# Expert weights in a mixture-of-experts kernel: from selector matmuls to a DRAM scratch and spreading DMAs

## The chip, the cores and the metric

The kernel runs on one core of one Trainium2 chip. Its engines are TensorE (PE; its weight loads are listed as PEld), VectorE (DVE), ScalarE (ACT), GpSimd (POOL) and SyncE (SP, which here only issues DMAs). The metric is the device time of one execution in microseconds, of which lower is better.

## What is computed

A network of four layers, each a cross-attention block and a feed-forward block with gated residuals, over x of 16 x 128 tokens with 128 features (2048 tokens). The feed-forward blocks of layers 0, 2 and 3 route tokens to experts. Cut to what matters:

```python
scores = sigmoid(x @ gate_weight.T)          # layers 0 and 3; layer 2: softmax
topk_idx = top_k(masked(scores), TOP_K)      # layer 0: 16 experts, 4 chosen; layer 3: 32, 6; layer 2: 8, 2
topk_w = topk_w / (topk_w.sum(-1) + 1e-20) * 2.5
combine = zeros((T, E)).at[arange(T)[:, None], topk_idx].add(topk_w)
y = sum over e of combine[:, e] * down_e(act(up_e(xn)))      # and one shared expert in layers 0 and 3
x = x + tanh(gate) * y
```

Experts have 64 hidden features in layers 0 and 3 and 128 in layer 2. Layer 3 has a second up projection per expert (silu(gate) * up).

## The kernel before, in words

The program is a row of stages; each is a block in which every engine has its own instruction stream, and semaphores order the streams. The three routed stages are `feed_forward` (L1394) with the tags f0, f2 and f3. Features lie on the 128 partitions and tokens along the free dimension. The tokens form 4 groups (NG) of 512 (GT). A tile is 128 hidden features, so two experts in f0 and f3 and one in f2; a group has J tiles: 10 in f0 (8 routed, 2 shared), 8 in f2, 17 in f3 (16 routed, 1 shared). Work is counted by n = g * J + j, N = 40, 32 and 68.

TensorE's order is written out by hand (L1504 to L1523). First come the router's logits (L1259), then `ahead` up projections (20 in f0, 16 in f2 and f3; L1456, and L1461 for the second one of f3), during which VectorE chooses the experts (`Route.choose`, L1296). `turn_back(0)` then transposes the weights of group 0 to expert-major form. After that, step m of the loop issues up(m + ahead), select(m), turn_back(m) for m = 1, 2, 3, and down(m - 2) (L1491). The last `ahead` steps have no up projection; the text calls them the tail.

The chosen weights leave `choose` in float32 and are split into three bf16 parts (L1388 to L1391), so that matmuls in bf16 move them exactly. `turn_back` multiplies the parts by an identity (L1276, four matmuls a group into bank 7), ScalarE copies the result to `combt` (`keep`, L1293), and `select(n)` (L1471) multiplies a matrix of ones and zeros, `sels`, by `combt`: the bank 4 or 5 then holds, on each partition, the weight of the expert to which this hidden feature belongs. VectorE's `weigh` (L1568) multiplies that PSUM bank by the activated hidden tile in the `ring` and writes h3, a ring of three buffers, which the down projection reads; `weigh(c)` waits for the down projection (in f2 for POOL's addition) of tile c - 3.

ScalarE activates every up projection into the ring (L1531) and in f3 copies the second one to `u` (L1537). POOL multiplies the two in f3 (L1617). In f2 the down matrix is the same for all experts, so POOL adds the 8 weighted tiles of a group (`accumulate`, L1632, seven additions), and one down projection a group follows. After a group's last down projection VectorE adds to x (L1576), takes statistics (L1582, L1588), POOL computes 1/sqrt(var) (L1645 to L1650), VectorE normalises (L1597) and TensorE turns the result (L1500); in TensorE's order this turn stands three steps behind the down projection. f3, the last stage, has none of this but stores x from SyncE (L1670).

`sels` is built by POOL: for f0 in the stage of L430, for f2 and f3 in pieces inside the attention stages before (`selector_piece`, L1209).

Of the kernel before, what the change touches and what calls it, by code (L numbers as in the profile page):

```python
# [77 lines left out]
class Kernel:  # L78


    def __init__(self, nc, ctx, dram, out):
# [35 lines left out]
        self.sels = sb("sels", [P, 2048], BF16)  # L117
        self.combt = sb("combt", [P, T], BF16)
# [295 lines left out]
def l0_queries_keys_values(k, lat_t, ctxn_t, qn, kl, kc, v):  # L414
# [9 lines left out]
         ("proj", "sq", "total", "root", "guard", "inv", "scaled", "turn", "copied", "sel")}  # L424
# [5 lines left out]
    with nc.Block() as block:  # L430
# [3 lines left out]

        @block.gpsimd
        def _(pool):
            pool.memset(k.combt[:, :], 0.0).then_inc(S["sel"], 1)
            make_selectors(pool, k, 16, 64, S["sel"], 1)
# [258 lines left out]
def small_head_attention(k, tag, sub, names, bias_q, bias_k, bv, bo, mask_rows, set_mask, weights_of, selectors):  # L697
# [20 lines left out]
          "inv", "on", "out", "added", "stated", "xb", "sel")}  # L718
# [14 lines left out]
    with nc.Block() as block:  # L733
# [100 lines left out]
        def _(pool):  # L834
            xv = k.x[:, :].rearrange("p (b c) -> p b c", b=NB)
            pool.memset(vp[:, :, :], 0.0).then_inc(S["zero"], 1)
            for b in range(NB + 1):
# [22 lines left out]
                if b >= 5 and (b - 5) % 2 == 0 and b < 13:  # L860
                    selector_piece(pool, k, *selectors, S["sel"], (b - 5) // 2)
# [347 lines left out]
def selector_piece(pool, k, experts, width, sem, piece):  # L1209

    s = k.sels[:, 0:experts * width].rearrange("p (e c) -> p e c", c=width)
    if piece == 0:
        pool.memset(k.sels[:, 0:experts * width], 0.0).then_inc(sem, 1)
        return
    pool.wait_ge(sem, piece)
    pool.affine_select(out=s, in_=s, compare_op=ALU.not_equal, fill=1.0, base=-(piece - 1) * experts,
                       pattern=[[-1, experts], [0, width]], channel_multiplier=1).then_inc(sem, 1)


def make_selectors(pool, k, experts, width, sem, n):  # L1220
    s = k.sels[:, 0:experts * width].rearrange("p (e c) -> p e c", c=width)
    pool.memset(k.sels[:, 0:experts * width], 0.0).then_inc(sem, 1)
    for part in range(3):
        pool.wait_ge(sem, n + part + 1)
        pool.affine_select(out=s, in_=s, compare_op=ALU.not_equal, fill=1.0, base=-part * experts,
                           pattern=[[-1, experts], [0, width]], channel_multiplier=1).then_inc(sem, 1)


class Route:
# [4 lines left out]
    def __init__(self, k, a, tag, E, groups, top_groups, top, kind, gate_w, rbias=None, factor=1.0):  # L1234
# [7 lines left out]
        self.s, self.w, self.low = take(E), take(E), take(E)  # L1242
# [3 lines left out]
        if groups:  # L1246
# [5 lines left out]
        self.parts = a.take((3 * NB * E + 1) // 2).bitcast(BF16).rearrange("p (t q e) -> p t q e", t=NB, q=3)  # L1252
        self.S = {n: k.sem(f"{tag}_" + n) for n in
                  ("logit", "st", "turn", "chain", "shift", "exp", "parts", "turn2", "comb")}
# [35 lines left out]
    def keep(self, act, g):  # L1290
        k, S, rows = self.k, self.S, 3 * self.E
        act.wait_ge(S["turn2"], g + 1)
        act.activation(k.combt[0:rows, g * GT:(g + 1) * GT], k.bank[7][0:rows, :], ACT.Copy)\  # L1293
           .then_inc(S["comb"], 1)

    def choose(self, dve):  # L1296
        k, S, E, G, best = self.k, self.S, self.E, self.G, self.best
        s, v, w, low, tot, base, rep, parts = (self.s, self.v, self.w, self.low, self.tot, self.base, self.rep,
                                               self.parts)
# [94 lines left out]
def feed_forward(k, tag, sub, tiles, function, ahead, one_down=False, routing=None, spare=(), bias=None):  # L1394
# [53 lines left out]
    with nc.Block() as block:  # L1448
        @block.tensor
        def _(pe):  # L1450
# [437 lines left out]
```

## Time and profile before

| | us |
|---|---|
| median of 3 runs (lowest to highest) | 1316.79 (1315.12 to 1317.58) |
| the profiled execution, own time | 1312.83 |
| its span, first to last instruction | 1311.0 |
| PE busy | 1142.2 (87%) |
| DVE busy | 765.1 (58%) |
| ACT busy | 682.4 (52%) |
| POOL busy | 364.4 (28%) |

The profile is of one execution, and all its times are counted from the span's start. f0 lies at about 140 to 242 us, f2 at 879 to 971, f3 at 1108 to 1311. Durations of matmuls include the fill of the pipeline, so that those of neighbours overlap; float32 matmuls are listed as two records each. What an instruction waited for stands in brackets behind it: idle time of the engine, and what ended it.

### The profile page before, as it was taken

The page shows a single profiled execution, that of the slowest core. Times are in us where ns is not written, and L with a number is a line of the kernel's source. Part 1 is how long each engine was busy: PE and PEld are TensorE (multiplying, and loading weights), DVE is VectorE, ACT ScalarE, POOL GpSimd, SP SyncE. Part 2 cuts the span into 40 slices and gives each one's busy share as a digit, 9 for nine tenths or more (in the row PEclk, how much of TensorE's full clock was granted, in tenths as well). Part 3 has the DMA queues.
Part 4 walks back from the last instruction along what each step waited for, and adds up shares of the span by engine and source line. Part 5 has one row for each costly group of instructions (what it writes and reads, how often), then busy time and mean ns, then how long its engine had stood idle before and what let it go on. Part 6 is the DMA issues. An engine that isn't in the chain of part 4 may idle for free. (4 is left out here: it accounts for less than half of the span.)

```text
span 1311.0 us, 24476 instructions
## 1 busy us (share of the span) xinstructions
PE 1142.2 (87%) x9697; PEld 838.0 (64%) x9697; DVE 765.1 (58%) x1671; ACT 682.4 (52%) x1205; POOL 364.4 (28%) x340
## 2 busy tenths in 40 slices
PE   1778898489999999999998599969439997999998
PEld 0567367478888888888885366643225664466667
DVE  5858535465656565656553379964537996722224
ACT  1677630165666666666654166656116665644441
POOL 3200001222222323232322422203662320744441
PEclk9999899699999999999999789989768997999999
DMA  4500000100000000000000000000000000000000
GB/s 166 189 1 1 0 1 1 65 1 1 1 1 1 1 1 1 1 2 1 1 2 1 0 2 2 2 1 0 0 0 2 2 2 2 1 0 8 9 0 17
DMA packets 6526, 16.27 MB, mean 12 GB/s; under 512 B 1312, under 2 KB 3568, under 8 KB 5520
## 3 DMA queue, kind: packets, MB, share of 16 engines
q1 hardware_dynamic: 6416, 14.74, 3.1%
q8 instruction: 77, 1.26, 0.4%
q14 instruction: 33, 0.27, 0.1%
HBM read 13.69 MB, written 1.05 MB: 11 GB/s over the span
## 5 line engine op out<-in xcount | busy, mean ns | idle before, releaser
L1099 POOL TENSOR_TENSOR work<-work 128x1024 f32<-128x1024 f32 x64 | 121.3, 1896 | 302.4 <-DVE work L1177 302.4
L1164 DVE TENSOR_REDUCE work<-psum 128x8 f32<-128x1024 f32 x64 | 78.0, 1219 | 93.0 <-PE psum L1000 93.0
L1116 ACT ACTIVATE work<-work 128x1024 f32<-128x1024 f32 x64 | 67.4, 1053 | 98.3 <-DVE work L1168 98.3
L1175 DVE TENSOR_REDUCE work<-work 128x8 f32<-128x1024 f32 x64 | 77.3, 1208 | 68.2 <-ACT work L1116 68.2
L1491 PEld LDWEIGHTS psum<-w_down,work 128*128 128x128 f32 x768 | 99.5, 191 | 24.4 <-issue 21.7
L887 ACT ACTIVATE work<-psum 128x512 f32<-128x512 f32 x128 | 72.8, 596 | 67.0 <-PE psum L777 66.1
L1491 PE MATMUL psum<-w_down,work 128*128 128x128 f32 x768 | 100.6, 275 | 0.7 <-DVE x L1576 0.7
L1568 DVE TENSOR_TENSOR work<-psum,big 128x512 f32<-128x512 f32 x67 | 45.8, 688 | 87.5 <-PE psum L1471 85.5
L919 DVE TENSOR_REDUCE work<-psum 128x8 f32<-128x1024 f32 x64 | 75.4, 1219 | 32.9 <-PE psum L765 18.8
L777 PEld LDWEIGHTS psum<-ident,work 128*128 128x128 f32 x512 | 57.4, 143 | 43.9 <-issue 30.7
L1168 DVE TENSOR_TENSOR work<-psum,work 128x1024 f32<-128x1024 f32 x64 | 78.4, 1225 | 6.4
L777 PE MATMUL psum<-ident,work 128*128 128x128 f32 x512 | 76.0, 282 | 6.3 <-ACT work L887 6.0
L1000 PEld LDWEIGHTS psum<-work 64*128 64x128 f32 x1024 | 59.6, 188 | 24.4 <-issue 23.5
L926 DVE TENSOR_TENSOR work<-psum,work 128x1024 f32<-128x1024 f32 x64 | 75.0, 1213 | 0.0
L884 ACT ACTIVATE work<-work 128x1024 f32<-128x1024 f32 x64 | 65.5, 1052 | 14.0 <-DVE work L926 13.0
L1120 ACT ACTIVATE work<-psum 128x512 f32<-128x512 f32 x128 | 69.2, 598 | 2.3 <-PE psum L1015 2.3
L1015 PE MATMUL psum<-ident,work 128*128 128x128 f32 x512 | 66.4, 273 | 0.9 <-ACT work L1120 0.9
L1456 PE MATMUL psum<-xnt,ctx_tok 128*128 128x512 f32 x128 | 66.6, 602 | 0.0
L1000 PE MATMUL psum<-work 64*128 64x128 f32 x1024 | 65.8, 278 | 0.7 <-ACT work L1111 0.7
L1461 PE MATMUL psum<-xnt,big 128*128 128x512 f32 x128 | 65.8, 595 | 0.0
L1645 POOL TENSOR_SCALAR work<-work 128x4 f32<-128x4 f32 x12 | 2.7, 228 | 217.5 <-DVE work L1588 217.5
L1032 PE MATMUL psum<-work 128*64 128x128 f32 x1024 | 63.0, 276 | 0.1
(319 smaller groups left out, 2544.5 us busy)
## 6 DMA issues: line engine op xcount, KB each, us to landing
x<-in_x SPq DMA_DIRECT2D x1, 1024.0 KB, 4.8
ctx_tok<-in_ctx SPq DMA_DIRECT2D x1, 1024.0 KB, 6.8
ctxt<-in_ctxt SPq DMA_DIRECT2D x1, 1024.0 KB, 10.3
mask<-in_mask SPq DMA_DIRECT2D x1, 1024.0 KB, 6.5
w_down<-in_down SPq DMA_DIRECT2D x1, 1024.0 KB, 7.0
ctx_tok<-in_g SPq DMA_DIRECT2D x1, 1024.0 KB, 4.9
big<-in_u SPq DMA_DIRECT2D x1, 1024.0 KB, 6.9
out<-x SPq DMA_DIRECT2D x4, 256.0 KB, 2.2
```

The source lines that it names most:

```text
L777: mm = pe.transpose(bank[4 + g % 2][:, i * P:(i + 1) * P], prob[:, b % 2, h * P:(h + 1) * P], k.ident[:, :])
L887: act.activation(probt[:, g, :], bank[4 + g % 2][:, :], ACT.Copy).then_inc(S["pt"], 1)
L919: dve.tensor_reduce(nmax[:, b % 2, 8 * half:8 * half + 8], s, AX.X, ALU.max, negate=True)\
L926: dve.tensor_tensor(prob[:, b % 2, half * 1024:(half + 1) * 1024] .rearrange("p (h c) -> p h c", c=P), s, nmax[:, b % 2, 8 * half:8 * half ...
L1000: mm = pe.matmul(bank[2 * half + r][:, c * P:(c + 1) * P], qt[rows, u % 2, at:at + P], kt[rows, u % 2, at:at + P], start=True, stop=True)
L1099: pool.tensor_tensor(prob[:, u % 2, h, :], prob[:, u % 2, h, :], rinv[:, u % 2, h].unsqueeze(2).broadcast_to([P, 8, P]), ALU.mult)\
L1116: act.activation(p, p, ACT.Exp).then_inc(S["exp"], 1)
L1120: act.activation(probt[:, t, :], bank[4 + t % 2][:, :], ACT.Copy).then_inc(S["pt"], 1)
L1164: dve.tensor_reduce(nmax[:, u % 2, h], s, AX.X, ALU.max, negate=True).then_inc(S["max"], 1)
L1168: dve.tensor_tensor(prob[:, u % 2, h, :], s, nmax[:, u % 2, h].unsqueeze(2).broadcast_to([P, 8, P]), ALU.add)\
L1175: dve.tensor_reduce(rsum[:, u % 2, h], prob[:, u % 2, h, :], AX.X, ALU.add).then_inc(S["sum"], 1)
L1491: mm = pe.matmul(y[g % 2][:, b * P:(b + 1) * P], h[:, b * P:(b + 1) * P], tiles[j][4], start=first and b == 0, stop=last, skip_group_check ...
```

## The change

The weights of the chosen experts stay float32. The splitting into three parts, the selector matrices and the selector matmuls are gone. `turn_back` transposes the float32 weights, `keep` copies them to a float32 `combt` of 32 partitions, and SyncE writes each group's rows to a DRAM tensor `chosen`. For every routed tile SyncE then reads the row (f2) or the two rows (f0, f3) of 512 weights from DRAM, spread over 128 or 64 and 64 partitions, into one of four SBUF buffers (`spread`, 256 KB a tile), and `weigh` reads its weights there. SyncE waits for a group's write before it reads, and for the multiply of tile c - 4 before it fills that tile's buffer again. The stores of f3 are issued between the reads.

```diff
-        self.sels = sb("sels", [P, 2048], BF16)
-        self.combt = sb("combt", [P, T], BF16)
+        self.combt = sb("combt", [32, T])
...
-        @block.gpsimd
-        def _(pool):
-            pool.memset(k.combt[:, :], 0.0).then_inc(S["sel"], 1)
-            make_selectors(pool, k, 16, 64, S["sel"], 1)
...
-                if b >= 5 and (b - 5) % 2 == 0 and b < 13:
-                    selector_piece(pool, k, *selectors, S["sel"], (b - 5) // 2)
...
     def turn_back(self, pe, g):
-        k, S, rows = self.k, self.S, 3 * self.E
+        k, S = self.k, self.S
         pe.wait_ge(S["parts"], 1)
         if g:
             pe.wait_ge(S["comb"], g)
         for c in range(GB):
-            mm = pe.matmul(k.bank[7][0:rows, c * P:(c + 1) * P],
-                           self.parts[:, GB * g + c, :, :].rearrange("p q e -> p (q e)"), k.ident16[:, :],
-                           start=True, stop=True)
+            mm = pe.transpose(k.bank[7][0:self.E, c * P:(c + 1) * P], self.w[:, GB * g + c, :], k.ident[:, :])
         mm.then_inc(S["turn2"], 1)
...
     def keep(self, act, g):
-        k, S, rows = self.k, self.S, 3 * self.E
+        k, S = self.k, self.S
         act.wait_ge(S["turn2"], g + 1)
-        act.activation(k.combt[0:rows, g * GT:(g + 1) * GT], k.bank[7][0:rows, :], ACT.Copy)\
+        act.activation(k.combt[0:self.E, g * GT:(g + 1) * GT], k.bank[7][0:self.E, :], ACT.Copy)\
            .then_inc(S["comb"], 1)
...
-            link(dve.tensor_tensor(w, w, wide(tot, E), ALU.mult))
-
-        link(dve.tensor_copy(parts[:, :, 0, :], w))
-        link(dve.tensor_tensor(low, w, parts[:, :, 0, :], ALU.subtract))
-        link(dve.tensor_copy(parts[:, :, 1, :], low))
-        dve.tensor_tensor(parts[:, :, 2, :], low, parts[:, :, 1, :], ALU.subtract).then_inc(S["parts"], 1)
+            dve.tensor_tensor(w, w, wide(tot, E), ALU.mult).then_inc(S["parts"], 1)
...
+    WR = 4
+    spread = a.take(WR * GT, "p (n c) -> p n c", n=WR) if routed else None
+    landed = [k.sem(f"{tag}_weights{n}") for n in range(WR)]
...
-            def select(n):
-                g, j = divmod(n, J)
-                if weighted[j]:
-                    c = made(n) - 1
-                    pe.wait_ge(r.S["comb"], g + 1)
-                    if c >= 2:
-                        pe.wait_ge(S["made"], c - 1)
-                    pe.matmul(bank[4 + c % 2][:, :], tiles[j][3], k.combt[:, g * GT:(g + 1) * GT],
-                              start=True, stop=True).then_inc(S["sel"], 1)
...
             for m in range(N + LAG + TURN + 1):
                 if m + ahead < N:
                     up(m + ahead)
-                if m < N:
-                    select(m)
                 if routed and 1 <= m < NG:
                     r.turn_back(pe, m)
...
-                dve.wait_ge(S["sel"], c + 1)
+                dve.wait_ge(landed[c % WR], 16 * len(tiles[n % J][3]) * (c // WR + 1))
                 wait_ready(dve, n)
...
-                dve.tensor_tensor(h3[:, c % 3, :], bank[4 + c % 2][:, :], ring[n % R], ALU.mult)\
+                dve.tensor_tensor(h3[:, c % 3, :], spread[:, c % WR, :], ring[n % R], ALU.mult)\
                    .then_inc(S["made"], 1)
...
-        if last_sub:
-            @block.sync
-            def _(sp):
-                for g in range(NG):
-                    sp.wait_ge(S["added"], g + 1)
-                    sp.dma_start(k.out[:, g * GT:(g + 1) * GT], k.x[:, g * GT:(g + 1) * GT])\
-                      .then_inc(S["stored"], 16)
+        @block.sync
+        def _(sp):
+            def store(g):
+                sp.wait_ge(S["added"], g + 1)
+                sp.dma_start(k.out[:, g * GT:(g + 1) * GT], k.x[:, g * GT:(g + 1) * GT]).then_inc(S["stored"], 16)
+
+            for n in weighted_tiles if routed else ():
+                g, j = divmod(n, J)
+                c = made(n) - 1
+                if g == 0 and j < NG:
+                    rows, of = slice(0, r.E), slice(j * GT, (j + 1) * GT)
+                    sp.wait_ge(r.S["comb"], j + 1)
+                    sp.dma_start(k.dram["chosen"][rows, of], k.combt[rows, of]).then_inc(r.S["kept"], 16)
+                    if j == 0:
+                        sp.wait_ge(r.S["kept"], 16)
+                if g == 1 and j == 0:
+                    sp.wait_ge(r.S["kept"], 16 * NG)
+                if c >= WR:
+                    sp.wait_ge(S["made"], c - WR + 1)
+                width = P // len(tiles[j][3])
+                for half, e in enumerate(tiles[j][3]):
+                    sp.dma_start(spread[half * width:(half + 1) * width, c % WR, :],
+                                 k.dram["chosen"][e:e + 1, g * GT:(g + 1) * GT].broadcast_to([width, GT]))\
+                      .then_inc(landed[c % WR], 16)
+                if last_sub and g and j == 8:
+                    store(g - 1)
+            if last_sub:
+                store(NG - 1)
                 sp.wait_ge(S["stored"], 16 * NG)
...
-            tiles = [(cut("up0", j), None, None, k.sels[:, j * P:(j + 1) * P], cut("down0", j))
+            tiles = [(cut("up0", j), None, None, (2 * j, 2 * j + 1), cut("down0", j))
                      for j in range(8)]
...
+    dram["chosen"] = nc.dram_tensor("chosen", (32, T), F32, kind="Internal").ap()
```

## Rows read from the trace of the kernel before

**Rows 1.** The page: busy us of each engine (share of the span) xinstructions.

```profile
PE 1142.2 (87%) x9697; PEld 838.0 (64%) x9697; DVE 765.1 (58%) x1671; ACT 682.4 (52%) x1205; POOL 364.4 (28%) x340
```

**Rows 2.** The selector matmuls: ns min/median/max, first and last start.

```profile
L1471 PE MATMUL psum<-combt,sels x128: 376/379/634, 162.9 to 1301.7; 128*128 128x512 bf16 x128
```

**Rows 3.** Timeline of PE in f3: start us, us, engine, line, out<-in.

```profile
1242.17 1.05 PE L1491 MATMUL psum<-w_down,work 128*128 128x128 f32 x8
...
1243.06 1.02 PE L1456 MATMUL psum<-xnt,ctx_tok 128*128 128x512 f32 x2
...
1243.92 1.02 PE L1461 MATMUL psum<-xnt,big 128*128 128x512 f32 x2
...
1244.78 0.38 PE L1471 MATMUL psum<-combt,sels 128*128 128x512 bf16 x1
...
1244.99 1.05 PE L1491 MATMUL psum<-w_down,work 128*128 128x128 f32 x8
```

**Rows 4.** Stretches: sum of busy us (x instructions) of PE PEld DVE ACT POOL, PEclk, DMA, GB/s.

```profile
930.00:947.00 17.00, 6.90 (x25) 3.59 (x24) 9.16 (x21) 0.60 (x1) 11.21 (x14) 0.66 0.00 0
```

**Rows 5.** Timeline of f2: start us, us, engine, line, out<-in [idle before <-releaser].

```profile
901.06 0.69 DVE L1568 TENSOR_TENSOR work<-psum,big 128x512 f32<-128x512 f32 x1 [10.86 <-PE psum L1471]
...
949.13 0.66 DVE L1568 TENSOR_TENSOR work<-psum,big 128x512 f32<-128x512 f32 x1
...
949.30 0.23 POOL L1645 TENSOR_SCALAR work<-work 128x4 f32<-128x4 f32 x1 [3.10 <-DVE work L1588]
...
954.50 6.89 POOL L1632 TENSOR_TENSOR work<-work 128x512 f32<-128x512 f32 x5 [1.53 <-DVE work L1568]
```

**Rows 6.** Timeline at the start of f0.

```profile
158.72 0.43 DVE L1391 TENSOR_TENSOR work<-work 128x256 bf16<-128x256 f32 x1
...
161.59 0.40 PE L1276 MATMUL psum<-ident,work 128*48 128x128 bf16 x4
...
162.19 0.58 ACT L1293 ACTIVATE combt<-psum 48x512 bf16<-48x512 f32 x1
...
163.30 0.69 DVE L1568 TENSOR_TENSOR work<-psum,ctx_tok 128x512 f32<-128x512 f32 x1 [4.15 <-PE psum L1471]
...
166.20 1.16 PE L1491 MATMUL psum<-w_down,work 128*128 128x128 f32 x8
```

**Rows 7.** Timeline of f0: ends of three groups, and the first turn of a result.

```profile
185.21 0.75 DVE L1576 SCALAR_TENSOR_TENSOR x<-psum,gate,x 128x512 f32<-128x512 f32 x1 [0.20 <-PE psum L1491]
...
191.06 0.66 PE L1500 MATMUL psum<-ident,work 128*128 128x128 f32 x4
...
203.38 0.75 DVE L1576 SCALAR_TENSOR_TENSOR x<-psum,gate,x 128x512 f32<-128x512 f32 x1 [0.20 <-PE psum L1491]
...
217.41 0.75 DVE L1576 SCALAR_TENSOR_TENSOR x<-psum,gate,x 128x512 f32<-128x512 f32 x1 [0.20 <-PE psum L1491]
```

**Rows 8.** DMAs: size and us to landing; an issue on SP; and two stretches.

```profile
w_wq<-in_wq SPq DMA_DIRECT2D x1, 512.0 KB, 3.2
...
out<-x SPq DMA_DIRECT2D x4, 256.0 KB, 2.2
...
39.00 0.42 SPq L205 DMA_DIRECT2D w_wk<-in_wk  x1
...
8.80:10.20 1.40, 0.00 (x0) 0.00 (x0) 0.58 (x1) 0.21 (x1) 1.26 (x2) 1.00 0.63 127
...
10.50:13.00 2.50, 0.00 (x0) 0.00 (x0) 2.18 (x12) 0.52 (x1) 0.88 (x2) 1.00 0.99 408
```

**Rows 9.** VectorE beside POOL: timeline of f3's start, and POOL's multiplies by line.

```profile
1131.90 1.27 POOL L1617 TENSOR_TENSOR negb<-negb,work 128x512 f32<-128x512 f32 x1 [0.45 <-ACT work L1537]
...
1132.01 1.70 DVE L1386 TENSOR_TENSOR work<-work 128x512 f32<-128x512 f32 x1
...
1135.20 0.69 DVE L1389 TENSOR_TENSOR work<-work 128x512 f32<-128x512 f32 x1
...
L1617 POOL TENSOR_TENSOR ctxt<-ctxt,work x12: 1262/1270/1685, 1135.3 to 1245.7; 128x512 f32<-128x512 f32 x12
```

More of the change, by code:

```diff
@@ L423, in l0_queries_keys_values @@
     S = {n: k.sem("l0p_" + n) for n in
-         ("proj", "sq", "total", "root", "guard", "inv", "scaled", "turn", "copied", "sel")}
+         ("proj", "sq", "total", "root", "guard", "inv", "scaled", "turn", "copied")}
     wq, wkv = k.w["wq0"], k.w["wkv0"]
@@ L717, in small_head_attention @@
          ("setup", "stepped", "zero", "proj", "k", "q", "v", "km", "vp", "score", "max", "sub", "exp", "turn", "pt", "pv",
-          "inv", "on", "out", "added", "stated", "xb", "sel")}
+          "inv", "on", "out", "added", "stated", "xb")}
     def fills(b):
@@ L1204, in _ @@
                     total(u, 1)
[L1209 to L1226, printed above, removed]
 class Route:
@@ L1241, in __init__ @@
         self.st = a.take(GT)
-        self.s, self.w, self.low = take(E), take(E), take(E)
+        self.s, self.w = take(E), take(E)
         self.base = take(E) if rbias is not None else self.s
@@ L1251, in __init__ @@
         self.tot, self.best = a.take(NB), take(8)
-        self.parts = a.take((3 * NB * E + 1) // 2).bitcast(BF16).rearrange("p (t q e) -> p t q e", t=NB, q=3)
         self.S = {n: k.sem(f"{tag}_" + n) for n in
-                  ("logit", "st", "turn", "chain", "shift", "exp", "parts", "turn2", "comb")}
+                  ("logit", "st", "turn", "chain", "shift", "exp", "parts", "turn2", "comb", "kept")}
     def logits(self, pe):
@@ L1350, in choose @@
             mark(rep, v, E, self.top)
-            link(dve.scalar_tensor_tensor(out=w, in0=rep[:, :, 0:E], scalar=self.MARK, in1=v[:, :, 0:E],
-                                          op0=ALU.is_equal, op1=ALU.mult))
+            dve.scalar_tensor_tensor(out=w, in0=rep[:, :, 0:E], scalar=self.MARK, in1=v[:, :, 0:E],
+                                     op0=ALU.is_equal, op1=ALU.mult).then_inc(S["parts"], 1)
         else:
@@ L1782, in build @@
             tiles = [(cut("ew2", j), k.cols[:, C_EB + j:C_EB + j + 1], None,
-                      k.sels[:, j * P:(j + 1) * P], w["comb2"][:, :]) for j in range(8)]
+                      (j,), w["comb2"][:, :]) for j in range(8)]
             k.stage(feed_forward, "f2", 5, tiles, ACT.Silu, ahead=16, one_down=True,
@@ L1789, in build @@
             k.stage(small_head_attention, "a3", 6, ("wq3", "wk3", "wv3", "wo3"), k.col("bq3"), k.col("bk3"),
-                    k.rows[:, R_BV3:R_BV3 + P], k.gated_bo[:, 1, :], k.key_mask_rows, k.set_key_mask, 3,
-                    (32, 64))
+                    k.rows[:, R_BV3:R_BV3 + P], k.gated_bo[:, 1, :], k.key_mask_rows, k.set_key_mask, 3)
         if stages > 7:
             k.stage(normalise, "n7", k.x, k.xn, k.xnt)
-            tiles = [(cut("g3", j), None, cut("u3", j), k.sels[:, j * P:(j + 1) * P], cut("down3", j))
+            tiles = [(cut("g3", j), None, cut("u3", j), (2 * j, 2 * j + 1), cut("down3", j))
                      for j in range(16)]
```

8 lines of the change are left out of this document (3 added, 5 removed).

## The prediction

> **What bounds the kernel now.** I read the page's engine totals first. TensorE is busy 87% of the span [rows 1], so taking work from it looks like gain, but an average over eight stages can't say where. The selector matmuls run in three stages only (tags f0, f2, f3), 128 in all, each listed at 0.379 us [rows 2]. That duration includes the pipeline's fill, so what one costs the stream must be read from start to start. I did that in the timeline of f3: select starts at 1244.78, the down projection behind it at 1244.99, and from one down to the next are 0.89 us of down, 0.86 and 0.86 of the two up projections and 0.21 of select: 2.82 us a tile with no gap [rows 3]. In the tail of a stage, where no up projections are left, it is 0.89 + 0.21 = 1.1. So here TensorE is the bound and a select is worth 0.213 us, no more.
>
> The table by stretches says where that doesn't hold: over one group of f2 TensorE is busy 6.90 of 17.00 us, at a granted clock of 0.66 [rows 4], between its two levels. There POOL's chain of additions (L1632) sets the pace: five in 6.89 us, one every 1.38 [rows 5]. A select removed there is worth nothing.
>
> **What goes.** f3: 64 x 0.213 = -13.6 us. f0: 32 x 0.213 = -6.8. f2: 32 x 0. The four casts and subtractions at the end of the choice go too, but the last one ends at 159.15 and the matmuls that turn the weights back start at 161.59, after up projections [rows 6], so VectorE was waited for by nobody: 0. In f3 they end just as TensorE arrives; that is also 0, since its up projections cover them. The selector building on POOL in the attention stages frees an engine that is not on the path there: 0 (at most a us of gain, if an instruction of another engine stood behind it).
>
> **The turn back in float32** replaces four bf16 matmuls by four float32 transposes. I price it at 0.1 us more for each of the 8 in f0 and f3, between 0 and 0.26 (the transposes of L1500 are listed at 0.66 for four, the bf16 ones at 0.40 [rows 6, 7], a part of which is fill): +0.4 a stage.
>
> **The new way of a weight.** Before: turn back, ScalarE's copy (0.58), select, multiply at 163.30; the first down starts at 166.20 [rows 6]. After: copy, a write to DRAM that SyncE waits for, then one or two reads, then the multiply. The write: 2.2 us from issue to landing, as the stores of the output [rows 8]. The read of 256 KB: no row shows one with these sources. The lower end: 512 KB into an idle queue landed in 3.2 us [rows 8]; 256 KB less at 408 GB/s [rows 8] is 0.6 less, 2.6. The upper end: the one broadcast of a 2 KB row over 128 partitions (mask0, 256 KB) was in transfer from 8.8 us, and while it was the queue moved 127 GB/s instead of 408 [rows 8]; at that rate 256 KB are 2.1 us, 4.0 to landing. The full rate is back from 10.5 us [rows 8], so the transfer can't have been much longer than 8.8 to 10.5; I take 1.6 us a tile in transfer and 3.6 to landing, since this is the nearest row, a broadcast too. SyncE pays 0.42 us for each issue [rows 8].
>
> *f0, start.* The copy ends at 162.8 [rows 6]; write landed at 165.0; second read issued at 165.5, landed at 169.2 at most, I take 168.7; multiply done at 169.4. TensorE, with the three selects gone, is at its first down at about 165.9 (166.20 before): it stands 3.5 us. Tile 3 pays again: its weights wait for the fourth turn back, which is queued in TensorE behind that first down, then for copy, write issue, reads (0.6 + 0.9 + 3.6) and multiply; between are two downs and two ups, 3.5 us, against about 5.2: 1.5 us more. Together +5.0.
> *f3, start.* The same chain is 0.3 us of waiting for ScalarE, 0.6 of copy, 6.6 as above (162.8 to 169.4) and some 0.6 of waiting for POOL (below), 8.1 from the end of the turn back; TensorE fills 3 x 1.72 of up projections and 0.9 of further turns, 6.1: +2.0. Tile 3 has 5.2 us of cover: nothing.
> *f2, start.* POOL's chain begins with the first multiply, at 901.06 before [rows 5]. After: the copy ends 0.5 us ahead of that as it did in f0, at 900.5; write 902.8, read 906.3: +5.2.
>
> **Tails.** Without up projections TensorE would take a tile in 0.89 us. SyncE's two issues are 0.84, four buffers with 3.6 + 0.7 + 0.1 us around give 1.1, the transfer 1.6. In f3 about seven tiles are already loaded or multiplied when its tail begins, nine loads remain (14.4 us and 2.5 behind the last): 17 us against 19.5 before, where the full 16 x 0.213 would give 16.1: +0.9. In f0 a group of the tail took 14.03 us (203.38 to 217.41 [rows 7]), of which 5.85 are add, statistics, POOL's root and normalising before TensorE can turn ([rows 7], 185.21 to 191.06). Selects inside that wait cover nothing. Of 3.4 us I leave 1.0: +2.4; and the first group's turn, which TensorE now reaches 0.6 us sooner while the root comes 0.3 to 0.5 later, waits +0.9.
>
> **The wait that the change adds without saying so.** VectorE's multiply read PSUM and SBUF; now it reads two operands in SBUF. The trace shows what that does beside POOL: a 128x512 multiply of two SBUF operands, started at 1132.01 while POOL's had run since 1131.90, took 1.70 us instead of the 0.69 of the one at 1135.20; it ended 0.54 beyond POOL's. The other way, POOL's multiply that came just behind the one at 1135.20 is the longest of its kind, 1.685 us against a median of 1.270 [rows 9]. They exclude each other. In f3 1.27 + 0.69 = 1.96 fits in 2.61 a tile; f0 has next to nothing on POOL. In f2 it doesn't fit: 1.26 + 0.61 = 1.87 a tile in place of 1.38. From the third addition of a group to its seventh: 5 x 0.49 = 2.45, four groups: +9.8. Further, after each group's statistics VectorE starts a multiply at 949.13 and POOL its root at 949.30 [rows 5]: the root now waits for it, 0.45 x 3 = +1.4. The Trainium skill (SBUF — State Buffer, Who interferes with whom) says that a VectorE instruction with two SBUF inputs contends with a GpSimd one that reads SBUF, whoever comes first holding the ports to its end. If instead only a VectorE instruction in a faster copy mode did so, as one might guess from casts alone, f2 would keep 1.38 a tile and the sum would be 11.2 lower.
>
> **Sum** against the profiled execution (span 1311.0, own time 1312.83): f0 -6.8 + 0.4 + 5.0 + 2.4 + 0.9 = +1.9. f2 +5.2 + 9.8 + 1.4 = +16.4. f3 -13.6 + 0.4 + 2.0 + 0.9 = -10.3. Total +8.0, 1320.8 for such an execution. That one was 3.96 us under the median of the runs, 1316.79, so for the median 1316.8 + 8.0, 1325.
>
> **Rivals.**
> 1. *Faster.* The ports are shared more kindly (VectorE multiplies two tiles ahead while POOL stands between groups, and slips between additions), and the broadcasts land in 2.6 us. Then f0 -1, f2 +4.2 and half of 11.2 (+9.8), f3 -13.6 + 0.4 + 1.2 = -12; a further us from POOL's freed attention stages: -4 to -5, 1312. It decides if POOL's pitch in f2 stays under about 1.6. For it: TensorE's gain in f3 is certain. Against it: VectorE's lead is cut to h3's three buffers, and a blocked instruction gets the ports in turn. If f2 kept its pace wholly, -10: 1307.
> 2. *Slower by far: the transfer becomes the bound.* At 2.1 us a tile or more (127 GB/s is 2.06), f2 goes at the pace of the reads, and f0's tail: 16 x 0.5 in f0, 28 x 0.25 to 0.5 in f2, 3 in f3: +18 more, 1343. For it: the one broadcast row in the trace. Against: only one, at the edge of another transfer; in f0 and f3 two rows are read, perhaps in parallel.
> 3. *No gain in f3.* POOL and VectorE together hold TensorE there as well, through the two buffers of u: +9 more, 1334. Against it: 1.96 under 2.61.
> 4. *Nothing to see:* start costs and gains cancel, 1314 to 1319.
>
> **How the numbers follow.** What a measurement of this kernel can tell from no change is 0.2%, 2.6 us. My forecast 0.52 (1320 to 1332 its own range), rival 1 0.25, rival 2 0.10, rival 3 0.05, rival 4 0.08. A part of the forecast's low end lies near no change: slower 0.60, same 0.13, faster 0.27. The range leaves out the far ends of rivals 1 and 2: 1309 to 1341.
>
> **What would show it.** The multiply (L1568 before) at 0.69 us in f0 but 1.2 to 1.9 in f2 beside POOL, POOL's additions at up to 1.9 there, five of them in over 9 us; f3's tile at 2.61; TensorE idle 3 to 4 us before the first down of f0, waiting for VectorE, which waits for a DMA; reads landing in 3 to 4 us. It is wrong if POOL's additions keep 1.26 and 1.38 apart (then faster), if VectorE waits for reads in the middle of f3 (then much slower), or if TensorE's tile in f3 doesn't fall by 0.21.

## The result and the profile after

The changed kernel takes 1337.12 us (median of 4 runs, 1336.26 to 1338.75), the kernel before 1316.59 beside it (1315.12 to 1317.58): ratio 1.0158, 95% interval 1.0141 to 1.0176, or +20.5 us. The forecast was +8.0. The sign held and the time lies inside the range, but the size was missed by 12.5 us. The profiled execution took 1336.26 us, its span is 1334.2.

The page of the kernel after (TensorE's total answers to [rows 1]; then the two kinds of read):

```profile
PE 1126.2 (84%) x9569; PEld 832.6 (62%) x9569; DVE 795.3 (60%) x1659; ACT 682.5 (51%) x1205; POOL 356.4 (27%) x327
...
work<-chosen SPq DMA_DIRECT2D x192, 128.0 KB, 3.1
work<-chosen SPq DMA_DIRECT2D x32, 256.0 KB, 3.6
```

TensorE has 16 us less to do, VectorE is listed 30 us busier although it has 12 instructions less, and the span grew by 23. Where the time went is read stage by stage, from the first router matmul to the additions to x that end each group (us; group 0 holds the stage's start too):

| stage | kernel | total | group 0 | 1 | 2 | 3 |
|---|---|---|---|---|---|---|
| f0 | before | 90.4 | 44.6 | 18.2 | 14.0 | 13.6 |
| f0 | after | 100.1 | 53.0 | 17.4 | 15.0 | 14.8 |
| f2 | before | 84.6 | 35.5 | 16.0 | 16.7 | 16.4 |
| f2 | after | 104.6 | 45.9 | 19.9 | 19.9 | 18.8 |
| f3 | before | 197.3 | 84.2 | 47.8 | 46.1 | 19.1 |
| f3 | after | 191.9 | 81.8 | 44.4 | 42.7 | 23.1 |

So f0 +9.7 (forecast +1.9), f2 +20.0 (+16.4), f3 -5.4 (-10.3); what lies between the stages -1.5. That is +22.8 between two profiled executions, whose own times differ by 23.4.

Some 3 us of it are not the change. The granted clock of a stage's first 10 us differs from execution to execution. First 10 us of f0, the kernel before and then the one after; then of f2, the kernel after and experiment 4, whose f0 and f2 are the changed kernel's (in each row, the third number from the end is the clock):

```profile
140.60:150.60 10.00, 10.00 (x28) 3.49 (x28) 4.61 (x28) 7.24 (x10) 0.00 (x0) 0.85 0.00 0
140.60:150.60 10.00, 10.00 (x25) 3.81 (x26) 3.26 (x20) 6.08 (x8) 0.00 (x0) 0.69 0.00 0
...
887.60:897.60 10.00, 6.33 (x19) 2.43 (x20) 4.33 (x41) 4.91 (x7) 0.00 (x0) 0.83 0.01 2
...
890.80:900.80 10.00, 6.38 (x23) 2.51 (x24) 5.93 (x60) 6.11 (x8) 0.00 (x0) 1.00 0.01 2
```

Experiments 1 and 2 leave f0 as it was before, and their profiles show 0.69 at its start too: group 0 takes 46.2 us there instead of 44.6, and with 0.89 granted in its third group 15.7 instead of 14.0, f0 93.7 in all. Experiment 4's f2 takes 103.0 instead of 104.6. So a difference of 1.6 us in the first group of a stage, or of 3.3 to 3.9 in a whole one (experiments 1 and 11), can be the clock's; the medians differ by 20.5 and not by 23.

**f3, where TensorE is the bound.** Timeline of the kernel after, to be held against [rows 3]:

```profile
1240.68 1.05 PE L1447 MATMUL psum<-w_down,work 128*128 128x128 f32 x8
1241.55 1.27 POOL L1571 TENSOR_TENSOR big<-big,work 128x512 f32<-128x512 f32 x1 [1.34 <-ACT work L1491]
...
1241.87 1.50 DVE L1522 TENSOR_TENSOR work<-work,negb 128x512 f32<-128x512 f32 x1 [1.11 <-PE psum L1447]
...
1243.29 1.05 PE L1447 MATMUL psum<-w_down,work 128*128 128x128 f32 x8
```

From one down projection to the next are 2.61 us; it was 2.82. The select was worth the 0.21 that the forecast read. VectorE's multiply starts 0.32 behind POOL's and lasts 1.50 instead of 0.69: 1.50 covers POOL's remaining 0.95 and 0.55 more. It costs nothing, since 2.61 holds both: TensorE is busy without a gap from 1218 to 1305.

**f2, where POOL is the bound.** Timeline of its second group, the kernel after, beside [rows 5]:

```profile
935.56 0.66 DVE L1522 TENSOR_TENSOR work<-work,negb 128x512 f32<-128x512 f32 x1
935.73 0.57 POOL L1599 TENSOR_SCALAR work<-work 128x4 f32<-128x4 f32 x1 [2.43 <-DVE work L1542]
...
941.29 10.03 POOL L1586 TENSOR_TENSOR work<-work 128x512 f32<-128x512 f32 x5 [1.53 <-DVE work L1522]
943.68 0.69 DVE L1522 TENSOR_TENSOR work<-work 128x512 f32<-128x512 f32 x1 [1.26 <-POOL work L1586]
945.62 0.69 DVE L1522 TENSOR_TENSOR work<-work 128x512 f32<-128x512 f32 x1 [1.26 <-POOL work L1586]
```

Five additions of POOL take 10.03 us instead of 6.89, and VectorE's multiplies come every 1.94. Each one waits 1.26 for POOL (it frees a buffer of h3), takes 0.69, and only then does POOL's next addition move: two engines in turn, 1.26 + 0.68. From one start to the next are 2.40 and then 1.94, where it was 1.41 before; the first group, which waits for reads, goes at 1.78 to 2.54. The root's first step is 0.57 instead of 0.23.

**The start of f0.** Timeline of the kernel after; [rows 6] had the first down at 166.20:

```profile
163.10 0.60 PE L1247 MATMUL psum<-ident,work 128*16 128x128 f32 x4
...
163.80 0.57 ACT L1262 ACTIVATE combt<-psum 16x512 f32<-16x512 f32 x1
...
164.39 0.31 SPq L1631 DMA_DIRECT2D chosen<-combt  x1
...
165.97 1.13 SPq L1640 DMA_DIRECT2D work<-chosen  x2
...
171.20 1.29 DVE L1522 TENSOR_TENSOR work<-work,ctx_tok 128x512 f32<-128x512 f32 x2 [11.99 <-DMA work<-chosen]
...
171.95 2.08 PE L1447 MATMUL psum<-w_down,work 128*128 128x128 f32 x8 [4.68 <-DVE work L1522]
...
173.81 1.91 PE L1422 MATMUL psum<-xnt,w_up 128*128 128x512 f32 x2
...
175.52 1.06 PE L1247 MATMUL psum<-ident,work 128*16 128x128 f32 x4
...
177.23 0.31 SPq L1631 DMA_DIRECT2D chosen<-combt  x1
...
181.09 0.69 DVE L1522 TENSOR_TENSOR work<-work,ctx_tok 128x512 f32<-128x512 f32 x1 [6.77 <-DMA work<-chosen]
```

TensorE stands for 4.68 us. Behind the stand its work takes twice as long: the down 2.08 instead of 1.05, the pair of ups 1.91 instead of 1.02, the four turns 1.06 instead of 0.60. The fourth turn back (175.52) stands in that queue, its weights are written at 177.23, and the fourth tile is multiplied at 181.09. The fourth down starts 9.1 us later than before (181.83 against 172.74), the first only 5.8 later. Stretches of the kernel after (sum of busy us and instructions of PE, PEld, DVE, ACT, POOL; granted clock; DMA share; GB/s):

```profile
171.90:176.00 4.10, 4.05 (x13) 2.67 (x14) 1.28 (x2) 0.24 (x1) 0.00 (x0) 0.50 0.16 43
181.00:193.00 12.00, 11.17 (x65) 8.21 (x66) 4.84 (x7) 3.61 (x7) 0.00 (x0) 1.00 0.82 182
...
953.00:992.00 39.00, 6.64 (x27) 5.15 (x25) 16.97 (x40) 1.19 (x2) 26.29 (x25) 0.50 0.25 68
...
1305.00:1325.00 20.00, 15.94 (x118) 14.95 (x117) 9.65 (x14) 0.00 (x0) 0.46 (x1) 0.91 0.67 155
```

The granted clock is 0.50 of full speed, 1.2 GHz, right after the stand: it fell before the stand ended (1.00 in 169 to 170, 0.50 from 171.0) and is full again from 178. Before the change the same 4.1 us were granted 1.00. In the second half of f2 it is 0.50 throughout (0.58 in the last two groups before); TensorE is busy 6.64 of those 39 us, and was busy 12.68 of 33.20. The other two rows are stretches in which VectorE waits for reads: 182 and 155 GB/s, where [rows 8] showed 408 for the loads at the start of the kernel.

### The profile page after: what moved, and what is told of

It reads as the page before. It is cut to its first block and busy times, and to the rows that moved or that the text cites. A ratio compares the mean times of both kernels' runs of the same rounds, so it can differ in the third digit from the quotient of the medians.

```text
span 1334.2 us, 24319 instructions
## 1 busy us (share of the span) xinstructions
PE 1126.2 (84%) x9569; PEld 832.6 (62%) x9569; DVE 795.3 (60%) x1659; ACT 682.5 (51%) x1205; POOL 356.4 (27%) x327
## 3 DMA queue, kind: packets, MB, share of 16 engines
q1 hardware_dynamic: 26768, 48.77, 12.5%
## 5 line engine op out<-in xcount | busy, mean ns | idle before, releaser
L1447 PEld LDWEIGHTS psum<-w_down,work 128*128 128x128 f32 x768 | 102.3, 202 | 45.1 <-issue 26.6
L1447 PE MATMUL psum<-w_down,work 128*128 128x128 f32 x768 | 105.4, 288 | 13.2 <-DVE work L1522 12.2
L1522 DVE TENSOR_TENSOR work<-work,big 128x512 f32<-128x512 f32 x67 | 63.3, 953 | 82.2 <-DMA work<-chosen 58.4
L911 DVE TENSOR_REDUCE work<-psum 128x8 f32<-128x1024 f32 x64 | 75.3, 1219 | 33.2 <-PE psum L759 18.8
L876 ACT ACTIVATE work<-work 128x1024 f32<-128x1024 f32 x64 | 65.5, 1052 | 15.1 <-DVE work L918 14.1
L1506 ACT ACTIVATE xnt<-psum 128x512 f32<-128x512 f32 x12 | 7.2, 598 | 114.5 <-PE psum L1456 114.5
```

The costliest lines, as they stand in the source:

```text
L911: dve.tensor_reduce(nmax[:, b % 2, 8 * half:8 * half + 8], s, AX.X, ALU.max, negate=True)\
L1447: mm = pe.matmul(y[g % 2][:, b * P:(b + 1) * P], h[:, b * P:(b + 1) * P], tiles[j][4], start=first and b == 0, stop=last, skip_group_check ...
```

## The experiments

The theory behind the forecast: port sharing costs f2, the chain write, read, multiply costs the starts, the transfer is too slow for TensorE's tails. The rivals for the part that was missed: the one DRAM row that all partitions read is slow; SyncE's issues are the bound; four buffers are too few.

**1. Only the second SBUF operand, in f2.** The kernel before keeps its selectors; the multiply of f2 reads four fixed SBUF stretches in place of PSUM.

```diff
-                dve.tensor_tensor(h3[:, c % 3, :], bank[4 + c % 2][:, :], ring[n % R], ALU.mult)\
+                held = k.ctxt[:, c % 4 * GT:(c % 4 + 1) * GT]
+                dve.tensor_tensor(h3[:, c % 3, :], held if sub == 5 else bank[4 + c % 2][:, :], ring[n % R], ALU.mult)\
```

> The kernel before, with every selector matmul kept, but in f2 alone the multiply takes its weight operand from a finished SBUF tensor instead of the PSUM bank (so f2's weights are wrong numbers and the selectors' results there go unread). No DMA is added. Theory (VectorE with two SBUF operands and POOL exclude each other): POOL's additions come 1.94 us apart instead of 1.38, five of them in 9.2 us instead of 6.9, the root waits 0.3 us behind VectorE; f2 is 10 to 13 us longer and the whole 1327 to 1330 us. Rival (what f2 lost in the change is the pace of the reads from DRAM): no change, 1316 to 1318 us.

1323.57 us (1321.47 to 1324.05), ratio 1.0052 [1.0032, 1.0072]. Less than was expected (10 to 13 us more in f2): f2 takes 92.5 instead of 84.6, +7.9. Timeline of f2 in this kernel:

```profile
932.29 5.52 DVE L1569 TENSOR_TENSOR work<-ctxt,work 128x512 f32<-128x512 f32 x4 [0.32 <-PE psum L1471]
933.95 3.31 POOL L1633 TENSOR_TENSOR work<-work 128x512 f32<-128x512 f32 x2 [0.63 <-DVE work L1569]
...
948.00 4.86 POOL L1633 TENSOR_TENSOR work<-work 128x512 f32<-128x512 f32 x3
```

A merged row runs from the first start to the last end, so the pitch is not its length divided by its count. The three additions from 948.00, each listed at about 1.53, start 1.67 apart; where POOL also waits 0.63 for the multiply that it adds, the starts are 1.79 to 1.90 apart. Only one pitch behind the first two additions of a group is longer (1.96). Here VectorE's multiply starts while POOL's addition still runs (0.23 to 0.48 behind its start), is listed at up to 1.76 us, and ends 0.55 behind POOL's end. In the changed kernel it is released by that end and takes its full 0.69 after it. So port sharing alone has more than one price, 0.26 to 0.49 a tile or 0.53 over the 1.41 from start to start before, by whether the multiply already stands at the port.

**2. The same in f3.**

```diff
+                held = k.xnt[:, c % 4 * GT:(c % 4 + 1) * GT]
+                dve.tensor_tensor(h3[:, c % 3, :], held if sub == 7 else bank[4 + c % 2][:, :], ring[n % R], ALU.mult)\
```

> The same in f3 alone (f3's weights are wrong numbers). Theory: VectorE's multiply is stretched from 0.69 to about 1.5 us, POOL's stays 1.27, both fit in TensorE's 2.82 us a tile, and the time doesn't move by more than 1 us, 1316 to 1318. Rival (the exclusion holds TensorE in f3 as well, through u and the ring): a tile above 2.9 us and 5 us or more in total.

1316.82 us (1315.75 to 1318.21), ratio 1.0003 [0.9992, 1.0013]; f3 197.5 against 197.3. No cost, so the rival that both engines together hold TensorE in f3 falls. The reason was partly another than expected: with the select in place the multiply kept 0.69 and POOL's became 1.36 instead of 1.27, since VectorE now comes first (it starts at 1243.65, POOL at 1244.11).

**3. Each partition reads its own DRAM row.** Same sizes and issues, another source.

```diff
-                                 k.dram["chosen"][e:e + 1, g * GT:(g + 1) * GT].broadcast_to([width, GT]))\
+                                 k.dram["x"][half * width:(half + 1) * width, g * GT:(g + 1) * GT])\
```

> The changed kernel, but each read takes as many bytes from as many different DRAM rows (64 or 128 rows of 2 KB of the input x) instead of one row of chosen for all partitions; so the weights are wrong numbers. Issues, waits and buffers are the same. Theory (reading one 2 KB row for all partitions is what limits the reads to about 178 GB/s): the engines move 350 to 400 GB/s, f3's last group falls from 23.1 us between the additions to x to 17 or 18, f0 loses 2 to 4 us, f2 about 1, in total 8 to 11 us less than the changed kernel: 1326 to 1329. Rival (SyncE's two issues a tile and the fixed time to landing set the pace): within 2 us of 1337, with the same landing of 3.1 us.

1335.69 us (1333.78 to 1338.28), ratio 1.0154 [1.0134, 1.0174]. The theory of the one slow row, which wanted 8 to 11 us, falls: it is 1.4 us, no more than these runs scatter. In the stretch table of this kernel:

```profile
181.00:193.00 12.00, 11.89 (x69) 8.83 (x70) 4.39 (x8) 3.58 (x6) 0.00 (x0) 1.00 0.63 190
```

190 GB/s instead of 182, with the DMA engines 63% busy instead of 82%. A packet from the common row takes longer, but that is not what limits the rate.

**4. Twelve buffers in f3.** Eight more of them lie in weights of an attention that is over.

```diff
-    WR = 4
+    WR = 12 if last_sub else 4
...
+    if last_sub:
+        slot += [k.w[name][:, n * GT:(n + 1) * GT] for name in ("wq1", "wk1", "wv1", "wo1") for n in range(2)]
```

> The changed kernel with 12 weight buffers in f3 instead of 4 (eight lie in the weights of layer 1, which are no longer used). Theory (f3's last group is bound by reads of 1.5 us a tile that could have been made in the 2.61 us a tile before it): the reads run ahead, f3's last group falls from 23.1 us to 16 or 17, and the whole from 1337 to 1330 or 1331. Rival (DMAs run no further ahead since SyncE or the waits on made hold them): 1336 to 1338.

1331.45 us (1326.97 to 1332.91), ratio 1.0104 [1.0079, 1.0128]; f3's last group 17.3 instead of 23.1, its other groups as they were. Waits of VectorE in that group, the kernel after and then this one:

```profile
1313.63 0.69 DVE L1522 TENSOR_TENSOR work<-work,big 128x512 f32<-128x512 f32 x1 [1.12 <-DMA work<-chosen]
...
1316.99 0.69 DVE L1522 TENSOR_TENSOR work<-work,big 128x512 f32<-128x512 f32 x1 [2.66 <-DMA work<-chosen]
```

```profile
1316.53 0.69 DVE L1525 TENSOR_TENSOR work<-w_wo,big 128x512 f32<-128x512 f32 x1 [0.20 <-PE psum L1450]
1317.42 0.69 DVE L1525 TENSOR_TENSOR work<-work,big 128x512 f32<-128x512 f32 x1 [0.20 <-PE psum L1450]
1318.74 0.69 DVE L1525 TENSOR_TENSOR work<-work,big 128x512 f32<-128x512 f32 x1 [0.62 <-DMA work<-chosen]
```

With four buffers VectorE waits for reads from the seventh of the group's sixteen routed tiles on (1310.27); with twelve it keeps TensorE's 0.89 until the fourteenth (1318.74), when the buffers filled in advance are used up.

**5. All four turns back behind the last up projections, ahead of the first tile**, in all three stages.

```diff
-            if routed:
-                r.turn_back(pe, 0)
+                if routed and n >= ahead - NG:
+                    r.turn_back(pe, n - ahead + NG)
...
-                if routed and 1 <= m < NG:
-                    r.turn_back(pe, m)
```

> The changed kernel with all four turn-backs (and ScalarE's copies) put between the last four up projections ahead of the loop, in all routed stages. Theory (f0 and f2 lose their start to the chain turn back, copy, write, reads, multiply, and f0 a second time because the fourth turn back stands behind the first down projection, all of it made longer by TensorE's clock falling to half during the stall): TensorE's wait before f0's first down falls from 4.7 us to 2 or less, the 6.8 us gap before the fourth multiply goes, f0's first group is 5 to 8 us shorter, f2's 2 to 3, f3's 0 to 1; in total 1326 to 1330 us. Rival (the pace of the reads sets f0's first group whatever the order): 1334 to 1337.

1322.04 us (1320.86 to 1323.32), ratio 1.0043 [1.0026, 1.0059]: 15 us under the changed kernel, more than expected. f0 90.2, f2 99.0, f3 191.3; against kernels with the changed order and nearly the same clock at the stage's start (f0 97.1 in experiment 6, f2 103.0 in experiment 4) the order is worth about 7 us in f0 and 4 in f2. Timeline of f0's start in this kernel:

```profile
159.16 0.31 SPq L1627 DMA_DIRECT2D chosen<-combt  x1
...
160.73 1.13 SPq L1636 DMA_DIRECT2D work<-chosen  x2
...
164.37 0.69 DVE L1518 TENSOR_TENSOR work<-work,ctx_tok 128x512 f32<-128x512 f32 x1 [7.73 <-DMA work<-chosen]
...
165.12 1.16 PE L1447 MATMUL psum<-w_down,work 128*128 128x128 f32 x8
```

The write starts 5.2 us earlier (1.1 of it because the stage does), TensorE still has up projections while it is under way, there is no stand, the clock stays at its upper level, and the fourth turn back is no longer behind a down. The read to its multiply takes 3.64 us here; the same read took 5.23 in the changed kernel (165.97 to 171.20).

**6. Selectors kept in f2 alone**, `direct` telling the two ways apart.

```diff
+    direct = routed and sub in (1, 7)
+    r = Route(k, a, tag + "r", direct=direct, **routing) if routed else None
```

> The changed kernel with f2 put back to bf16 parts, selector matmuls and a PSUM operand; f0 and f3 stay with DMAs. Theory (f2 lost 20 us and the stages are independent): 1316 to 1319 us, f2 back at 84.6 us from its start to its last addition to x, POOL's additions 1.38 us apart. Rival (part of what f2 shows is passed on by the stages before it, as a lower clock): 1320 or more.

1318.14 us (10 runs, 1313.71 to 1319.82), ratio 1.0011 [1.0001, 1.0022]. f2 is back at 84.3; f0 97.1 and f3 192.4 keep what the change did to them (f0's first group lies between 50.1 and 53.0 in the kernels that have it as the change made it). By the medians, 19 of the 20.5 us of loss were f2's.

**7. f3 alone by DMA, with twelve buffers and early turns back.** `direct` for `sub in (7,)`, and the edits of 4 and 5.

> The kernel before in f0 and f2; in f3 alone the weights come by DMA, with 12 buffers and the turn-backs ahead of the loop. Theory (f3 gains 0.213 us for each of 64 selects and loses only its start): f3 is 11 to 13 us shorter than in the kernel before, 1303 to 1306 us in total, faster than both kernels. Rival (the reads at 1.5 us a tile or the start still cost 4 us or more): 1308 to 1312.

1304.99 us (1304.79 to 1310.54), ratio 0.9924 [0.9899, 0.9948]: faster than both. Its last group takes 19.1, more than the 17.3 of experiment 4. SyncE's queue in this kernel has a long gap:

```profile
1261.35 1.08 SPq L1712 DMA_DIRECT2D w_wv<-chosen  x2
...
1277.05 0.34 SPq L1695 DMA_DIRECT2D out<-x  x1
...
1277.44 1.10 SPq L1712 DMA_DIRECT2D w_wv<-chosen  x2
```

Between 1262.4 and 1277.0 it issues nothing: it stands at the store of the group before, whose place in the program (behind tile 8) comes up long before its result exists, and the reads wait behind it. Experiment 4 has the same gap (1293.4 to 1308.0) and its last group took 17.3, so the gap is not what sets the two apart. What differs is seen after it: here two read issues take 1.79 and 1.89 us instead of 0.6, and the store lands in 4.5 us instead of 2.3. Why stays open.

**8. One issue a tile, own rows.** Experiment 3 with one DMA of 128 rows in place of two of 64.

```diff
-                for half, e in enumerate(tiles[j][3]):
...
+                sp.dma_start(spread[:, c % WR, :], k.dram["x"][:, g * GT:(g + 1) * GT]).then_inc(landed[c % WR], 16)
```

> The changed kernel with 128 different DRAM rows per tile, as in the run with own rows, but read by one DMA of 128 partitions in f0 and f3 as well instead of two of 64 (the weights are wrong numbers). Theory (with own rows SyncE's two issues, some 1.1 us a tile, set the pace): f3's last group falls from 22.4 us to 18 or less and f0 by 2 to 4, in total 1327 to 1331 us. Rival (the round trip of four buffers, 3 us to landing each, sets it): within 2 us of 1335.7.

1332.99 us (1331.39 to 1334.21), ratio 1.0124 [1.0107, 1.0141]: 2.7 us under experiment 3 by the medians, 3.9 by the ratios (they ran in different rounds), between what the theory and the rival wanted. f3's last group 21.1 against 22.4, so halving SyncE's work is a small part of what is missing against 17.3. The Trainium skill (DMA: Bandwidth & Descriptors, Rules for kernel authors) says that two transfers to two halves of the partitions serialise and one of 128 is to be taken; the 2.7 us agree in sign.

**9. Stores later.** Experiment 7 with the store of the group before issued at the last routed tile's reads.

```diff
-                if last_sub and g and j == 8:
+                if last_sub and g and j == J - 2:
```

> As the run with DMAs in f3 alone (12 buffers, early turn-backs), but the stores of x for the groups before are issued at tile 15 of the next group instead of tile 8. Theory (with 12 buffers SyncE stands at the store, which waits for the addition to x, while buffers are free: the reads of the last group pause from about 1262 to 1277): the last group falls from 19.1 us to 16 or 17, and the whole from 1305.0 to 1302 or 1303. Rival (the reads at 163 to 170 GB/s are the bound and resume late whatever the store): 1305.

1302.89 us (1301.77 to 1305.48), ratio 0.9905 [0.9888, 0.9921]. Last group 16.4, 2.7 less than in experiment 7, SyncE's reads without the gap:

```profile
1262.32 3.70 SPq L1712 DMA_DIRECT2D w_wv<-chosen  x4
...
1267.54 3.70 SPq L1712 DMA_DIRECT2D w_wo<-chosen  x4
...
1272.76 8.93 SPq L1712 DMA_DIRECT2D work<-chosen  x8
```

Against the 19.1 before the change that is 2.8 of the 3.4 that sixteen selects are worth.

**10. Selects added to f2 that nobody reads.** The changed kernel with 32 matmuls of the select's size in f2; VectorE waits for them as it did for the selects.

```diff
+                if routed and (not direct or sub == 5) and m < N:
+                    select(m)
```

> The changed kernel (weights by DMA in all three stages), but in f2 TensorE also issues the 32 selector matmuls in their old place and VectorE waits for them as before; their result isn't read. Theory (in the changed kernel each multiply is released by the end of one of POOL's additions and takes the ports ahead of the next, 1.27 + 0.67 = 1.94 us a tile; paced by the selects it is issued while POOL runs and needs only 0.39 behind it, as in the run with two SBUF operands, 1.66): f2's later groups fall from 19.9 to about 18 us, f2 as a whole by 4 to 6 us, though work was added: 1331 to 1333 us. Rival (1.94 comes from the reads landing in SBUF or from their pace): groups of 19.9 us again and 1337 or more.

1332.19 us (1331.46 to 1333.46), ratio 1.0124 [1.0107, 1.0141]. More work made f2 5.5 us faster (99.1; its groups 1 to 3 take 17.9, 18.2 and 17.9, as in experiment 1, where the changed kernel's take 19.9, 19.9 and 18.8). Its timeline:

```profile
945.54 1.27 POOL L1648 TENSOR_TENSOR work<-work 128x512 f32<-128x512 f32 x1 [0.63 <-DVE work L1584]
945.84 3.79 DVE L1584 TENSOR_TENSOR work<-work 128x512 f32<-128x512 f32 x3 [0.37 <-PE psum L1484]
947.44 1.64 POOL L1648 TENSOR_TENSOR work<-work 128x512 f32<-128x512 f32 x1 [0.63 <-DVE work L1584]
...
961.50 6.54 POOL L1648 TENSOR_TENSOR work<-work 128x512 f32<-128x512 f32 x4
```

VectorE's multiply again starts while POOL runs (0.30 behind it), and the pitch is that of experiment 1: 1.90 in the first rows, 1.67 in the last. With it the 20.0 us of f2 fall into three parts: the second SBUF operand at its kinder price (experiment 1, 7.9), the other rhythm in groups 1 to 3 (4.6), and 7.5 in the first group. Of these 7.5 the first multiply is 5.9 late against experiment 1, 1.9 of it going with the clock at the stage's start (it is 4.0 late here, where that clock is 1.00), and the rest are waits for reads.

**11. f0 and f3 by DMA, f2 by selectors**, with early turns back, twelve buffers in f3 and the later stores.

> DMAs in f0 and f3 with early turn-backs, 12 buffers in f3 and the later stores; selectors in f2. It tells what the change is worth in f0 once its start is mended. Theory (f0 gains about 1.5 us in its first group and 0.7 in its second, and gives back 2 to 3 us in its two tail groups, where four buffers can't cover the reads): within 2 us of the run with DMAs in f3 alone and the later stores. Rival (6.8 us of selects come off f0 once it starts in time): 4 us or more faster than that run.

1300.69 us (1299.82 to 1303.88), ratio 0.9886 [0.9868, 0.9905]: the best version of this study, 1.1% under the kernel before. f0 takes 90.4, as before the change; f2 88.3, f3 182.1. Against experiment 9 the medians differ by 2.2 us, and f0, the only stage that the edit changes, gives nothing of that in the profiles. What moves there is unchanged code under another clock: f3's first group is 78.8 instead of 81.0, with 1.00 granted in its first 10 us instead of 0.77, and f2 takes 88.3 instead of 84.4, with 0.84 and 0.83 in its first 20 us instead of 1.00. So 2 us between these two are not to be explained.

## Why the forecast was right in sign and wrong in size

**Right.** The select is worth 0.21 us where TensorE is the bound: 2.82 to 2.61 a tile in f3, and its two middle groups 3.45 shorter each, 16 x 0.213 = 3.4. It is worth nothing in f2. A multiply of two SBUF operands and POOL exclude each other, and that costs f2 and not f3 (experiments 1, 2 and 10; experiment 6 shows f2 whole again with selectors). The Trainium skill's rule on the shared port (SBUF — State Buffer, Who interferes with whom) held: two SBUF inputs contend, and the one behind is blocked, not slowed (VectorE's multiply listed at 1.50 instead of 0.69 behind POOL's, POOL's addition at 1.80 instead of 1.26 behind VectorE's). VectorE waits for reads in tails and in the first groups only, not in the middle of f3. Rival 3 is out (experiment 2); rival 1 is out, for its point of decision was a pitch under 1.6 and it was 1.94 (1.78 to 2.54 in the first group); rival 2's bandwidth was not as bad as 127 GB/s, and not by its mechanism (experiment 3).

**Wrong, term by term** (forecast, measured):

- *f3's tail, +0.9.* The last group should have gained 3.4 - 0.9 = 2.5 and lost 4.0: a miss of 6.5, the largest. The step that failed is the one that prices the reads of the tail: "about seven tiles are already loaded or multiplied when its tail begins, nine loads remain (14.4 us and 2.5 behind the last)". When the group before ends (1305.3), six are multiplied, loaded or under way and ten remain. The first of the ten is issued at 1306.68, 1.4 us later, since SyncE refills a buffer only when its multiply is done, and the last lands at 1325.57: 18.9 us, 1.9 a tile, where the step had nine at 1.6. With 2.8 behind the last that makes the 23.1. In the tail the reads run at 155 GB/s with 4.3 us to landing. Twelve buffers give 5.8 of it back (experiment 4); one issue for two gives 1.3 (experiments 3 and 8). The store in SyncE's queue, which the diff put between the reads, was not in my sum at all: the longest wait of the tail, 2.66 us, is for the first tile read behind it, and with twelve buffers and early turns back its place cost 2.7 (experiments 7 and 9). What it costs with four buffers was not tried.
- *f0's start, +5.0.* The first group with its start came out 8.4 longer, where the sum had 3.7 for it (5.0 + 0.4 for the turns back, less 1.7 for its selects). 1.6 of the miss is the clock at the stage's start: ScalarE's copy ended at 164.37 and not at 162.8. Two things were not in the step. The second read landed 4.7 us behind its issue and not 3.2 (5.2 from the first read to the multiply). And TensorE, which stood for 4.7 us, came back at half its clock, so that the fourth turn back, which was queued behind the first down, came later still. My step had the queueing (1.5 us) but at the full clock: from the first down to the fourth the delay grew from 5.8 to 9.1 us. Experiment 5 shows that it comes from the order: f0 takes 90.2 there, with 0.83 granted in its first 10 us.
- *f0's tail, +2.4 and +0.9.* The three groups behind the first are 47.2 us against 45.8; -0.21 x 8 for each (8 routed tiles a group) and these two terms made -1.8. A miss of 3.2. VectorE waits 3.9 us for reads in the last two of them, though the engines are busy only 36 to 38% of the time there; those two groups were also granted 0.89 instead of 1.00, and as experiment 1 shows 15.7 us instead of 14.0 for the third group at 0.89 with no edit in f0, a part of the miss is the clock's. The parts were not told apart.
- *f2's start, +5.2.* The first multiply came 28.0 us behind the stage's start instead of 22.1: +5.9. With the clock at the stage's start as before it is +4.0 to +4.2 (experiments 10 and 4), so this term was a little high.
- *f2's additions, +9.8 and root, +1.4.* 20.0 - 5.9 = 14.1 against 11.2. The pitch was 1.94 and not 1.87, since nothing of the two overlaps when each is released by the other's end; but 1.38 before was 6.89 divided by five, and the starts were 1.41 apart, so the surplus of a tile, 0.53, is near the 0.49 of the sum. The root lost 0.34 a group and not 0.45, 1.0 in all. What the step had wrong is the first group: its surplus behind the first multiply is 4.5 where the term had 2.45, because its additions wait for reads as well (starts up to 2.54 apart). The others' surplus is 3.9, 3.2 and 2.4.
- *f3's start, +2.4 with the turn back.* The first group became 2.5 shorter where I had 1.0: this term was too high. Why was not tried; the clock in the stage's first 10 us was 0.82 and not 0.77, which can be a part of it.

Together f0 7.8, f2 3.6, f3 4.9 too little and 1.5 less between the stages: 14.8, and 8.0 + 14.8 = 22.8, the measured difference of the two profiled executions. About 3 us of it are the clocks at the stage's starts and not steps of the forecast. That the time still lies inside the stated range is owed to its width: it had been drawn for a slower transfer (rival 2), which is not what happened.

## What to carry to other kernels

An operand that moves from PSUM to SBUF is a change for the engine next door: if POOL sets the pace, count the multiply's full length into its pitch (1.26 + 0.68 in f2). A transfer that replaces matmuls pays in the steady part of a stage and is paid for at its ends, so before it is put in, the producer belongs ahead of the last cover (turns back early), the buffers must last for the tail, and nothing that waits may stand before it in its queue. Use it by stage, where TensorE is the bound: here f3 alone with those three edits gave -1.0%, f0 and f3 -1.1%, all stages without them +1.6%.

## What the runs showed of the hardware

- VectorE and POOL on the shared port have more than one rhythm: POOL's additions start 1.67 us apart when VectorE's multiply already stands at the port (it ends 0.55 behind POOL's), up to 1.90 when POOL also waits for that multiply, 1.94 when the multiply is released by the end of POOL's. Adding 32 matmuls that nobody reads, which shifted the release, saved 4.6 us in the three groups with that rhythm, and the whole kernel became 4.9 us faster.
- Reads of 2 KB rows, up to four tiles in flight, moved 155 to 190 GB/s where VectorE waited for them, however the source lay; loads of whole weights had shown 408 [rows 8]. The Trainium skill (DMA: Bandwidth & Descriptors, Anatomy of one DMA — SWDGE (gpsimd) path) gives 2.0 us and bytes at 436 GB/s, measured on another path of issue; an estimate by it is 2.3 us for 128 KB and 2.6 for 256 KB. Measured were 3.1 and 3.6. Why the rate is lower stays open; the common row is not the reason (experiment 3).
- The first read of f0 took 5.2 us to its multiply in the changed kernel, 4.7 to 5.0 in experiments 3, 4, 6 and 10, and 3.6 in experiments 5 and 11, with the same issues in nearly the same distances. Not settled.
- In a stand of TensorE of 4.7 us the granted clock fell to 1.2 GHz before the stand ended, and the first 5.6 us of work behind it were done at that level. With the same code, the clock granted in the first 10 us of f0 was 0.69 in some profiles and 0.85 in others, and that of f2 0.83 or 1.00; each pair differs by 1.6 us in the stage's first group.
- Not tried: a deeper h3 in f2, which might keep VectorE's multiply at the port and bring 1.94 to 1.66 without them; reads issued from a second queue.
